# Routing moved into the attention stage: tables, routing, empty-row stores and the first expert's weights, with one block fewer

## Chip, cores and metric

One core of one Trainium2 chip. The metric is the device time in microseconds (us) of one execution of the whole kernel, given as the median of several runs.

## The reference, cut to what matters

The kernel computes one tower block for 32 sequences of 512 tokens with 256 features: an embedding lookup, a two-directional Mamba layer, then attention and a mixture of experts. The last part is what the change touches:

```
x = layer_norm(h1).reshape(-1, 256)                 # 16384 rows
top_p, top_i = top_k(softmax(x @ router_weight), 2) # 8 experts, 2 for each row
order = argsort(top_i.reshape(-1), stable=True)     # rows of an expert, in the order of tokens
within = arange(N * K) - offsets[sorted_exp]        # a row's place in its expert's list
valid = within < cap                                # cap = ceil(N * K / E * 1.25): later rows are dropped
xt = padded_tokens.reshape(E, cap, H)
fc2 = einsum('ecf,efh->ech', gelu(einsum('ech,ehf->ecf', xt, moe_w1)), moe_w2)
moe_out = zeros((N, H)).at[padded_tid].add(fc2 * padded_probs)
out = h1 + moe_out
```

## The kernel before, in words

The program is a row of blocks. In a block each engine has its own instruction stream, written out by hand, and engines meet through semaphores; at a block's end all engines meet at a barrier. The blocks are the Mamba stage, `attention_stage`, `routing_stage` and `expert_stage`.

**`attention_stage`** (from L982) goes over 32 chunks of 512 rows, unrolled in Python (attention runs along the axis of 32 sequences; a chunk is 16 of the 512 positions with their 32 rows each). GpSimd (`@block.gpsimd`) first writes masks and small tables, then computes the scales of the layer norms (`scales1`, `scales2`), normalises the attention weights, adds the residual (`base`) and sends rows (`send`): for a chunk, eight indirect DMAs that put its rows, once for each of two chosen experts, into the DRAM tensor `expert_in` (`xd_dram`), where each expert has its own region of rows. `send(c)` runs two chunks behind. SyncE (SP) loads rows of later chunks into a ring of four and stores results. TensorE's `turn2` transposes the second layer norm's rows, `router` makes the logits, and `ranks` counts how many rows before this one chose each expert. VectorE's `keep_logits`, `pick_experts`, `next_rows` and `place` work out the choice and the row in `expert_in`; `place` writes the index tile `idx`, of which there is one, so its cast (L1651) waits until the chunk before has been sent and has landed. ACT's `second_odds` makes the weight of the second choice from the logits' difference. After the last chunk a tail repeats these steps for chunks 30 and 31 with nothing left to overlap.

**`routing_stage`** (L1714) finds, from the choices of all tokens kept in `both_all`, which rows fall within an expert's capacity, and a plan: how many blocks of 512 rows each expert has, and where the rows end. GpSimd builds 128x128 tables (`same`, `later`, `below`) with 48 instructions, each waiting for the one before; TensorE multiplies them with `both_all`; VectorE scans, compares, counts (`few`), and writes `plan` and the threshold `kept`.

**`expert_stage`** fills a zero tile, stores a block of empty rows behind each expert's rows (SP, L1923, eight stores at places read from `plan`) and one behind the output (L1925), waits for all nine, and then runs the turns: for each expert so many blocks of 512 rows as the plan says, 68 in this run. A turn loads rows (L1934), transposes them, applies the layer norm's weights on ACT (`move`, L2061), splits them into a high and a low part on VectorE, multiplies with `w1` (L2022), applies gelu, multiplies with `w2` (L2034), and adds the results to the output by indirect DMA (L1983). Expert weights are loaded by GpSimd into two sets; `weights_high` rounds them on ACT, and VectorE makes the low part (L2148, L2152, L2155). Each engine keeps its own loop through `experts`, which reads the count of an expert from `plan`.

## Time and profile before

| | |
|---|---|
| median of 3 runs | 4369.67 us (4357.84 to 4372.54) |
| the profiled execution | 4369.69 us |
| its span, from the first to the last instruction | 4368.2 us |
| busy: TensorE matmul (PE), weight load (PEld) | 91%, 68% of the span |
| busy: VectorE (DVE), ScalarE (ACT), GpSimd (POOL) | 84%, 65%, 53% |
| mean granted TensorE clock | 0.906 of full speed (2.4 GHz) |

Times in the rows are microseconds from the span's start, in one profiled execution. A bracket at the end of a line tells how long the engine stood idle before the instruction, and what ended the wait. The busy shares are averages over stages that differ much; a stage has to be read by itself.

### The profile page before, as it was taken

The page shows a single profiled execution, that of the slowest core. Times are in us where ns is not written, and L with a number is a line of the kernel's source. Part 1 is how long each engine was busy: PE and PEld are TensorE (multiplying, and loading weights), DVE is VectorE, ACT ScalarE, POOL GpSimd, SP SyncE. Part 2 cuts the span into 40 slices and gives each one's busy share as a digit, 9 for nine tenths or more (in the row PEclk, how much of TensorE's full clock was granted, in tenths as well). Part 3 has the DMA queues.
Part 4 walks back from the last instruction along what each step waited for, and adds up shares of the span by engine and source line. Part 5 has one row for each costly group of instructions (what it writes and reads, how often), then busy time and mean ns, then how long its engine had stood idle before and what let it go on. Part 6 is the DMA issues. An engine that isn't in the chain of part 4 may idle for free. (4 is left out here: it accounts for less than half of the span.)

```text
span 4368.2 us, 69821 instructions
## 1 busy us (share of the span) xinstructions
PE 3962.4 (91%) x19212; PEld 2959.7 (68%) x19213; DVE 3654.4 (84%) x7005; ACT 2853.2 (65%) x4732; POOL 2325.2 (53%) x1953
## 2 busy tenths in 40 slices
PE   6999999999999999999999869999999389999998
PEld 4666566666666666666656547777877278888987
DVE  7999999999999999999999858887888356666666
ACT  5777777777777777777777746666666145554444
POOL 2454545444454545445454536666666435555555
PEclk8989989898889989898999879988899689999999
DMA  2122211221222222222222212222222155555555
GB/s 68 45 44 42 52 38 45 42 52 42 47 47 42 46 41 48 42 49 44 42 52 39 40 45 82 83 81 75 79 81 75 63 123 96 97 105 96 87 96 85
DMA packets 197949, 272.58 MB, mean 62 GB/s; under 512 B 23377, under 2 KB 142546, under 8 KB 197842
## 3 DMA queue, kind: packets, MB, share of 16 engines
q0 software_dynamic: 94720, 131.65, 17.2%
q1 hardware_dynamic: 99680, 137.43, 11.2%
q10 hardware_dynamic: 3442, 2.21, 0.2%
q8 instruction: 50, 0.82, 0.1%
q14 instruction: 57, 0.47, 0.0%
HBM read 121.07 MB, written 150.14 MB: 62 GB/s over the span
## 5 line engine op out<-in xcount | busy, mean ns | idle before, releaser
L608 PE MATMUL pj<-xt,win 128*128 128x512 f32 x3144 | 919.0, 452 | 13.6 <-DVE uc L793 10.5
L608 PEld LDWEIGHTS pj<-xt,win 128*128 128x128 f32 x3144 | 674.9, 217 | 200.2 <-issue 46.9
L1983 POOL DMA_INDIRECT out<-e_y,e_to x272 | 461.2, 1696 | 367.9 <-ACT e_y L2089 308.2
L300 POOL TENSOR_TENSOR r<-r,neg_half 128x4 f32<-128x4 f32 x64 | 90.9, 1420 | 844.5 <-ACT r L383 844.5
L793 DVE SCALAR_TENSOR_TENSOR uc<-pj,convw,uc 128x511 f32<-128x511 f32 (+2 forms) x780 | 516.8, 728 | 4.9 <-ACT uc L407 4.9
L656 PE MATMUL po<-yz,wout 128*128 128x512 f32 x1024 | 483.6, 628 | 28.3 <-ACT fb L486 28.3
L325 POOL TENSOR_TENSOR wk<-v,uc 128x512 f32<-128x512 f32 x260 | 333.0, 1281 | 246.4 <-DVE v L841 245.6
L2034 PE MATMUL e_p<-e_w,e_a 128*128 128x256 f32 x3264 | 408.7, 282 | 1.9 <-DVE e_a L2144 1.9
L656 PEld LDWEIGHTS po<-yz,wout 128*128 128x128 f32 x1024 | 198.6, 199 | 310.5 <-issue 308.6
L2022 PE MATMUL e_p<-e_xt,e_w 128*128 128x512 f32 x1632 | 390.7, 396 | 5.6 <-DVE e_w L2148 3.0
L2034 PEld LDWEIGHTS e_p<-e_w,e_a 128*128 128x128 f32 x3264 | 386.2, 188 | 12.5 <-DVE e_a L2144 6.6
L2022 PEld LDWEIGHTS e_p<-e_xt,e_w 128*128 128x128 f32 x1632 | 304.3, 190 | 71.0 <-issue 7.4
L329 POOL TENSOR_TENSOR tp<-wk,bb 128x512 f32<-128x512 f32 x260 | 332.8, 1280 | 30.5 <-POOL wk L325 19.8
L2142 DVE CAST e_a<-e_af 128x512 fp32r<-128x512 f32 x272 | 118.3, 435 | 240.2 <-ACT e_af L2082 234.4
L677 PE MATMUL po<-wfus,fo 128*128 128x256 f32 x1024 | 238.1, 386 | 75.2 <-ACT fo L477 75.2
L1218 POOL DMA_INDIRECT expert_in<-a_xs,a_idx x256 | 249.8, 976 | 94.4 <-issue 80.0
L677 PEld LDWEIGHTS po<-wfus,fo 128*128 128x128 f32 x1024 | 189.3, 190 | 151.4 <-ACT fo L477 128.2
L848 DVE TENSOR_TENSOR_SCAN tp<-y,tp 128x512 f32<-128x512 f32 x256 | 291.8, 1198 | 0.0
L2082 ACT ACTIVATE e_af<-e_p 128x512 f32<-128x512 f32 x272 | 162.3, 598 | 185.2 <-PE e_p L2022 183.9
L833 DVE SCALAR_TENSOR_TENSOR wk<-wk,lg 128x1024 f32<-128x1024 f32 x130 | 222.6, 1712 | 71.3 <-ACT lg L463 71.3
L2089 ACT ACTIVATE e_y<-e_p,e_share 128x256 f32<-128x256 f32 x272 | 114.4, 472 | 234.8 <-PE e_p L2034 234.8
L415 ACT ACTIVATE zs<-pj 128x512 f32<-128x512 f32 x260 | 155.7, 599 | 168.9 <-PE pj L608 168.9
(247 smaller groups left out, 9076.3 us busy)
## 6 DMA issues: line engine op xcount, KB each, us to landing
e_x<-expert_in SPq DMA_DIRECT2D x138, 260.0 KB, 2.6
bb<-bc SPq DMA_DIRECT2D x65, 512.0 KB, 5.3
h_rows<-fb POOLq DMA_DIRECT2D x64, 512.0 KB, 6.3
h_rows<-h0c SPq DMA_DIRECT2D x32, 512.0 KB, 2.9
a_h<-h_rows SPq DMA_DIRECT2D x128, 128.0 KB
out<-a_bs SPq DMA_DIRECT2D x128, 128.0 KB
bc<-xd SPq DMA_DIRECT2D x65, 128.0 KB, 2.2
e_w1s<-in_moe_w POOLq DMA_DIRECT2D x10, 512.0 KB, 5.8
```

The lines of the kernel that those rows point to most:

```text
L325: pool.tensor_tensor(wk[:, m, :], v[:, m, :], uc[d][:, m, :], ALU.mult).then_inc(S["dtu_ok"], 1)
L329: pool.tensor_tensor(tp[:, m, :], wk[:, m, :], bb[d][:, 0, :], ALU.mult).then_inc(S["tp_ok"], 1)
L608: i = mm(pj[m][:], win[d][wp][:, k, c:c + P], xt[xp][:, k, :], start=(k == 0 and n == 0), stop=(k == KD - 1 and n == 2))
L656: i = mm(po[k][:], wout[d][:, m, k * P:(k + 1) * P], yz[:, m, :], start=(m == 0), stop=(m == MD - 1))
L677: i = mm(po[h][:, jj * DM:(jj + 1) * DM], fo[:, k, j * P:(j + 1) * P], wfus[d][:, k, :], start=(k == 0), stop=(k == KD - 1))
L793: stt(uc[d][:, m, to], pj[m][:, of], convw[d][:, m, tap:tap + 1], uc[d][:, m, to], ALU.mult, ALU.add).then_inc(S["cv"], 1)
L833: stt(wk[:, mm, :], wk[:, mm, :], 1.0, lg[:, mm, :], ALU.subtract, ALU.subtract).then_inc(S["g_ok"], 1)
L848: nc.vector.tensor_tensor_scan(tp[:, m, step], y[:, m, step], tp[:, m, step], 0.0, ALU.mult, ALU.add).then_inc(S["h_ok"], 1)
L1218: pool.indirect_dma_start(out=xd_dram, out_offset=bass.IndirectOffsetOnAxis(ap=idx[:, k, j:j + 1].bitcast(U32), axis=0), in_=xs[c % SENDS] ...
L1983: pool.indirect_dma_start(out=out, out_offset=bass.IndirectOffsetOnAxis(ap=to[n][:, j:j + 1].bitcast(U32), axis=0), in_=y[n][:, j, :], in_ ...
L2022: o = mm(p1[m][:], w1[i][wp][:, k, m * P:(m + 1) * P], xt[xp][:, k, :], start=(k == 0 and s == 0), stop=(k == KD - 1 and s == 2))
L2034: o = mm(p2[n][:, j, :], a[ap][:, m, (n * HT + j) * P:(n * HT + j + 1) * P], w2[i][wp][:, m, :], start=(m == 0 and s == 0), stop=(m == MF ...
```

## The change

The routing block is gone. Its parts go into the attention block, and some of what the expert block did first goes there too. The tiles that both blocks use (`plan`, `expert`, `kept`, the identity, the zero tile, both sets of weights) and a semaphore `emptied` are now made once outside and passed in as `moe`.

- GpSimd builds the routing tables and fills the zero tile after the first two calls of `scales1`. The constant rows that VectorE wrote one column at a time become two iotas. The identity is shared: the copies that the routing and the expert block built are gone.
- SP loads expert 0's weights after slot 2, and stores the empty block behind the output after slot 3 and waits for it. After its last slot it stores the eight empty blocks, as soon as the plan is there, and waits for the first of them; the other seven are waited for in the expert block, before expert 1's rows are read.
- ACT rounds expert 0's weights at the end of its stream.
- TensorE and VectorE: `ranks(30)` comes ahead of the last `turn2`, and `next_rows(30)`, `place(30)` ahead of `keep_logits(31)`. The routing products follow `ranks(31)`, and VectorE's routing follows `place(31)`, with the plan made before the scans. The first expert's low half is made there.
- The expert block starts without those steps. GpSimd loads only expert 1's weights there.

```diff
         @block.sync
+            def expert_weights():
+                for dst, name, of in ((moe.w1s, "moe_w1", "(k p) f -> p k f"), (moe.w2s, "moe_w2", "(m p) c -> p m c")):
+                    rows = DM if name == "moe_w1" else FF
+                    sp.dma_start(dst[0][:], w[name][0:rows, :].rearrange(of, p=P)).then_inc(S["ld_e"], 16)
+
+            def empty_rows():
+
+                sp.wait_ge(S["plan_ok"], 1)
+                for e in range(NE):
+                    row = sp.value_load(moe.plan[0:1, 1, e:e + 1], min_val=0, max_val=NE * X_ROWS - PAIR)
+                    sp.dma_start(xd_dram[bass.ds(row, PAIR), :].rearrange("(p j) c -> p j c", p=P), moe.zero[:]
+                                 ).then_inc(S["zst"] if e == 0 else moe.emptied, 16)
             for c in range(NCH + 1):
                 slot(c)
+                if c == 2:
+                    expert_weights()
+                if c == 3:
+                    sp.wait_ge(S["tab"], TABLES_R)
+                    sp.dma_start(out[NSEQ * SEQ:NSEQ * SEQ + PAIR, :].rearrange("(p j) c -> p j c", p=P),
+                                 moe.zero[:, :, 0:DM]).then_inc(S["zst"], 16)
+                    sp.wait_ge(S["zst"], 16)
+            empty_rows()
+            sp.wait_ge(S["zst"], 32)
+            sp.wait_ge(S["ld_e"], 32)
...
         @block.gpsimd
             scales1(0)
             scales1(1)
+            routing_tables()
...
         @block.scalar
             second_odds(NCH - 1)
+            act.wait_ge(S["ld_e"], 32)
+            act.activation(moe.w1[0][0][:], moe.w1s[0][:], ACT.Copy).then_inc(S["hi_ok"], 1)
+            act.activation(moe.w2[0][0][:], moe.w2s[0][:], ACT.Copy).then_inc(S["hi_ok"], 1)
...
         @block.tensor
+            ranks(NCH - 2)
             turn2(NCH - 1, True)
-            ranks(NCH - 2)
+            pe.wait_ge(S["rt"], ROUTES * (NCH - 2) + PICKS + 2)
             router(NCH - 1)
             pe.wait_ge(S["lg_ok"], NCH)
-            pe.wait_ge(S["rt"], ROUTES * (NCH - 2) + PICKS + 2)
             ranks(NCH - 1)
+            def routing():
+                pe.wait_ge(S["tab"], TABLES_R)
+                pe.wait_ge(S["rt"], ROUTES * (NCH - 1) + PICKS)
+                pe.wait_ge(S["hh_ok"], 2 * NCH)
+                pe.wait_ge(S["x2t_ok"], KD * NCH)
+                flat = both_all[:].rearrange("p t e -> p (t e)")
+                for i in range(2):
+                    cols = slice(SEQ * i, SEQ * (i + 1))
+                    mm(A[i][:], same[:], flat[:, cols], start=True, stop=True)
+                    mm(A[2 + i][:], later[:], flat[:, cols], start=True, stop=True)
+                pe.wait_ge(S["tot_ok"], 1)
+                mm(B[0][:, 0:NE], below[:], total[:], start=True, stop=True)
+                mm(B[0][:, NE:2 * NE], onef[:], total[:], start=True, stop=True).then_inc(S["counted"], 1)
+                pe.wait_ge(S["few_ok"], 1)
+                mm(B[1][:, 0:NE], onef[:], few[:], start=True, stop=True).then_inc(S["kept_ps"], 1)
...
         @block.vector
             normalise2(NCH - 1)
-            keep_logits(NCH - 1)
             next_rows(NCH - 2)
             place(NCH - 2)
+            keep_logits(NCH - 1)
             pick_experts(NCH - 1)
             next_rows(NCH - 1)
             place(NCH - 1)
+            def routing():
+                nc.vector.tensor_reduce(total[:], both_all[:].rearrange("p t e -> p e t"), AX_X, ALU.add
+                                        ).then_inc(S["tot_ok"], 1)
...
+                nc.vector.tensor_copy(moe.plan[:], planf[:]).then_inc(S["plan_ok"], 1)
...
 def expert_stage
         @block.sync
-            sp.wait_ge(S["zeroed"], 2)
-
-            for e in range(NE):
-                row = sp.value_load(plan[0:1, 1, e:e + 1], min_val=0, max_val=NE * X_ROWS - PAIR)
...
-            sp.wait_ge(S["zst"], 16 * (NE + 1))
+            def all_emptied(pair, i, q):
+
+                if i == 1:
+                    sp.wait_ge(emptied, 16 * (NE - 1))
...
         @block.gpsimd
-            load_weights(0, 0)
             load_weights(1, 1)
...
         @block.scalar
-            weights_high(0, 1)
             for n in range(2):
                 move(0, n)
...
         @block.vector
-            dve.wait_ge(S["hi_ok"], 1)
-            tt(w1[0][1][:], w1s[0][:], w1[0][0][:].bitcast(F32), ALU.subtract).then_inc(S["w1_ok"], 1)
+            dve.nop().then_inc(S["w1_ok"], 1)
```

The new function on GpSimd; the part left out is the 42 copies, multiplications and selects of before, each of which waits for the one ahead:

```
            def routing_tables():
                n = 0
                for tile, value in ((same, 0.0), (later, 0.0), (below, 0.0), (onef, 1.0)):
                    pool.memset(tile[:], value).then_inc(S["tab"], 1)
...
                pool.iota(row0[:], [[X_ROWS, NE]], base=0, channel_multiplier=0,
                          allow_small_or_imprecise_dtypes=True).then_inc(S["tab"], 1)
                pool.iota(steps[:], [[PAIR, MAX_PAIRS - 1]], base=PAIR, channel_multiplier=0,
                          allow_small_or_imprecise_dtypes=True).then_inc(S["tab"], 1)
                pool.memset(zero[:], 0.0).then_inc(S["tab"], 1)
                n += 3
                pool.wait_ge(S["tab"], n)
                pool.iota(zero[:, :, TOKEN], [[1, PAIR // P]], base=NSEQ * SEQ, channel_multiplier=PAIR // P,
                          allow_small_or_imprecise_dtypes=True).then_inc(S["tab"], 1)
```

The end of VectorE's routing, after the scans and additions that make `rank`:

```
                nc.vector.tensor_reduce(few[:], inside[:].rearrange("p t e -> p e t"), AX_X, ALU.add
                                        ).then_inc(S["few_ok"], 1)
                dve.wait_ge(S["hi_ok"], 1)
                tt(moe.w1[0][1][:], moe.w1s[0][:], moe.w1[0][0][:].bitcast(F32), ALU.subtract).then_inc(S["low_ok"], 1)
                dve.wait_ge(S["kept_ps"], 1)
                ts(moe.kept[:], inside_of, -0.5, None, ALU.add).then_inc(S["seq"], 1)
```

## Rows read from the trace of the kernel before

**Rows 1.** Stretches: length; busy PE, PEld, DVE, ACT, POOL (instructions); PE clock, DMA share, GB/s.

```profile
2524.00:3410.00 886.00, 815.47 (x5375) 676.89 (x5376) 711.49 (x2471) 550.78 (x957) 549.01 (x591) 0.90 0.22 75
3410.00:3516.41 106.41, 17.49 (x88) 13.11 (x88) 26.31 (x139) 8.79 (x14) 38.38 (x80) 0.56 0.29 103
3516.41:3531.40 14.99, 14.99 (x80) 13.01 (x81) 9.21 (x23) 5.50 (x11) 2.05 (x3) 0.79 0.31 102
3531.40:4340.00 808.60, 803.68 (x5271) 722.08 (x5270) 543.24 (x1465) 404.32 (x806) 458.30 (x278) 1.00 0.57 95
```

**Rows 2.** Timeline, tail of the attention block: start, length, engine, line, operation.

```profile
3421.15 0.19 ACT L1308 ACTIVATE a_odds<-a_gap 128x4 f32<-128x4 f32 x1
...
3425.54 0.16 DVE L1642 TENSOR_SCALAR a_whole<-a_odds 128x4 f32<-128x4 f32 x1
...
3427.17 1.06 POOL L1218 DMA_INDIRECT expert_in<-a_xs,a_idx  x1 [6.27 <-DVE a_flag L1613]
...
3438.66 0.17 DVE L1651 CAST a_idx<-a_dest 128x8 int32<-128x8 f32 x1 [7.53 <-DMA expert_in<-a_xs,a_idx]
...
3438.96 0.16 DVE L1658 TENSOR_TENSOR a_xs<-a_first,a_xs 128x4 f32<-128x4 f32 x1
3439.90 0.96 POOL L1218 DMA_INDIRECT expert_in<-a_xs,a_idx  x1 [2.81 <-DVE a_xs L1658]
...
3448.75 0.96 POOL L1218 DMA_INDIRECT expert_in<-a_xs,a_idx  x1 [0.30 <-issue]
```

**Rows 3.** One line's instructions: GpSimd's queue at the attention block's end (ns, start).

```profile
L995 POOLq DRAIN  x1: 2506/2506/2506, 3451.4 to 3451.4; - x1
```

**Rows 4.** Timeline of the routing block.

```profile
3454.20 1.98 DVE L1792 TENSOR_REDUCE r_total<-both_all 128x8 f32<-128x1024 f32 x1 [15.08 <-PEq L995]
...
3468.37 2.08 PE L1781 MATMUL r_ps<-both_all,r_same 128*128 128x512 f32 x2 [38.26 <-POOL r_below L1769]
...
3473.39 0.28 PE L1784 MATMUL r_pb<-r_total,r_below 128*128 128x8 f32 x2
...
3474.01 1.53 DVE L1810 TENSOR_TENSOR_SCAN r_rank<-r_ones,r_ps 128x64 f32<-128x64 f32 x8 [16.77 <-PE r_pb L1785]
...
3482.82 0.41 DVE L1832 TENSOR_TENSOR r_over<-r_pb,r_steps 128x248 f32<-128x248 f32 x1
...
3483.97 0.16 DVE L1843 CAST plan<-r_planf 1x16 int32<-1x16 f32 x1
3484.05 0.15 DVE L1846 TENSOR_SCALAR kept<-r_pk 128x8 f32<-128x8 f32 x1
```

**Rows 5.** Timeline of the expert block up to its first product.

```profile
3484.70 0.96 POOL L1948 MEMSET e_zero<- 128x1040 f32 x1 [16.38 <-POOLq L1719]
...
3486.70 1.23 POOL L1957 DMA_DIRECT2D e_ln<-in_ln  x2 [0.24 <-issue]
3486.86 10.91 SPq L1923 DMA_DIRECT2D expert_in<-e_zero  x8
...
3491.41 1.28 ACT L2054 ACT_TABLE_LOAD   x1 [61.93 <-DMA e_ln<-in_ln]
...
3498.01 1.23 DVE L2155 TENSOR_TENSOR e_w<-e_w1s,e_w 128x1024 fp32r<-128x1024 f32 x1 [13.81 <-ACT e_w L2067]
3508.96 6.83 SPq L1934 DMA_DIRECT2D e_x<-expert_in  x4
...
3512.93 1.93 ACT L2061 ACTIVATE e_xf<-e_pt,e_ln 128x256 f32<-128x256 f32 x4 [14.00 <-PE e_pt L2003]
...
3516.41 8.64 PE L2022 MATMUL e_p<-e_xt,e_w 128*128 128x512 f32 x24 [2.67 <-DVE e_xt L2136]
```

**Rows 6.** Timeline of GpSimd at the start of the attention block.

```profile
2570.35 4.10 POOL L1204 TENSOR_TENSOR a_ss<-a_ss,a_rs 128x512 f32<-128x512 f32 x4 [24.43 <-DVE a_rs L1551]
```

**Rows 7.** DMA issues from 3480 to 3520: count, size, median us to landing.

```profile
expert_in<-e_zero SPq DMA_DIRECT2D x8, 520.0 KB, 9.1
...
e_w2s<-in_moe_w POOLq DMA_DIRECT2D x3, 512.0 KB, 8.3
```

More of the change, by code:

```diff
@@ L11 @@
 import numpy as np
+from collections import namedtuple
 from contextlib import ExitStack
@@ L981, with attention_stage @@
 TABLES = 11 + NQ + 2 + 2 * NE + NQ
-NT = NSEQ * SEQ // P
+NTILE = NSEQ * SEQ // P
+FF = 512
+MF = FF // P
+CAP = -(-NSEQ * SEQ * TOP * 5 // (NE * 4))
+HALF = 256
+HT = HALF // P
+MAX_PAIRS = NSEQ * SEQ // PAIR
+TABLES_R = 4 + 16 + 10 + 16 + 4
+ExpertTiles = namedtuple("ExpertTiles", "plan expert kept ident zero emptied w1s w2s w1 w2")
 MASKED = -2.0 ** 127
-def attention_stage(nc, w, h1_dram, out, xd_dram, both_all):
+def attention_stage(nc, w, h1_dram, out, xd_dram, moe):
     ctx = ExitStack()
@@ L1038, in attention_stage @@
         lgc = sb("a_lgc", [P, TT, NE])
-        expert = sb("a_expert", [P, NE])
+        expert = moe.expert
         seen = sb("a_seen", [P, NE])
@@ L1058, in attention_stage @@
         xs = [sb(f"a_xs{i}", [P, TT, XW]) for i in range(SENDS)]
+        block_shape = [P, NTILE, NE]
+        both_all = sb("r_both", block_shape)
+        same = sb("r_same", [P, P])
+        later = sb("r_later", [P, P])
+        below = sb("r_below", [P, P])
+        onef = sb("r_ones", [P, P])
+        row0 = sb("r_row0", [P, NE])
+        steps = sb("r_steps", [P, MAX_PAIRS - 1])
+        rank = sb("r_rank", block_shape)
+        inside = sb("r_inside", block_shape)
+        total = sb("r_total", [P, NE])
+        few = sb("r_few", [P, NE])
+        over = sb("r_over", [P, NE, MAX_PAIRS - 1])
+        turns = sb("r_turns", [P, NE])
+        planf = sb("r_planf", [1, 2, NE])
+        zero = moe.zero
         A = [ctx.enter_context(nc.psum_tensor(f"a_pa{i}", [P, SEQ], F32)) for i in range(4)]
@@ L1718, in routing_stage, with expert_stage @@
+            routing()
+def expert_stage(nc, w1_dram, w2_dram, lnw_dram, xd_dram, out, moe):
     ctx = ExitStack()
@@ L1721, in sb @@
             return ctx.enter_context(nc.sbuf_tensor(name, shape, dt))
-        block_shape = [P, NTILE, NE]
-        ident = sb("r_ident", [P, P])
-        same = sb("r_same", [P, P])
-        later = sb("r_later", [P, P])
-        below = sb("r_below", [P, P])
-        ones = sb("r_ones", [P, P])
-        row0 = sb("r_row0", [P, NE])
-        steps = sb("r_steps", [P, MAX_PAIRS - 1])
-        rank = sb("r_rank", block_shape)
-        inside = sb("r_inside", block_shape)
-        total = sb("r_total", [P, NE])
@@ L1734, in routing_stage @@
-        few = sb("r_few", [P, NE])
-        over = sb("r_over", [P, NE, MAX_PAIRS - 1])
-        turns = sb("r_turns", [P, NE])
-        planf = sb("r_planf", [1, 2, NE])
-        ps_same = [ctx.enter_context(nc.psum_tensor(f"r_ps{i}", [P, SEQ], F32)) for i in range(2)]
-        ps_part = [ctx.enter_context(nc.psum_tensor(f"r_pp{i}", [P, SEQ], F32)) for i in range(2)]
-        ps_base = ctx.enter_context(nc.psum_tensor("r_pb", [P, 2, NE], F32))
-        ps_kept = ctx.enter_context(nc.psum_tensor("r_pk", [P, NE], F32))
@@ L1775, in _ @@
-        @block.tensor
-        def _(pe):
-            pe.wait_ge(S["tab"], TABLES_R)
-            flat = both_all[:].rearrange("p t e -> p (t e)")
-            for i in range(2):
-                cols = slice(SEQ * i, SEQ * (i + 1))
-                nc.tensor.matmul(ps_same[i][:], same[:], flat[:, cols], start=True, stop=True)
-                nc.tensor.matmul(ps_part[i][:], later[:], flat[:, cols], start=True, stop=True)
-            pe.wait_ge(S["tot_ok"], 1)
-            nc.tensor.matmul(ps_base[:, 0, :], below[:], total[:], start=True, stop=True)
-            nc.tensor.matmul(ps_base[:, 1, :], ones[:], total[:], start=True, stop=True).then_inc(S["counted"], 1)
-            pe.wait_ge(S["few_ok"], 1)
-            nc.tensor.matmul(ps_kept[:], ones[:], few[:], start=True, stop=True).then_inc(S["kept_ps"], 1)
@@ L1851 @@
-TABLES_R = 6 + 16 + 10 + 16
-def expert_stage(nc, w1_dram, w2_dram, lnw_dram, xd_dram, out, plan, expert, kept):
-    ctx = ExitStack()
-    with ctx:
-        def sb(name, shape, dt=F32):
-            return ctx.enter_context(nc.sbuf_tensor(name, shape, dt))
-        ident = sb("e_ident", [P, P])
+        plan, expert, kept, ident, zero, emptied, w1s, w2s, w1, w2 = moe
         ln = sb("e_ln", [P, 2, KD])
-        w1s = [sb(f"e_w1s{i}", [P, KD, FF]) for i in range(2)]
-        w2s = [sb(f"e_w2s{i}", [P, MF, DM]) for i in range(2)]
-        w1 = [[sb(f"e_w1{i}{h}", [P, KD, FF], F32R) for h in range(2)] for i in range(2)]
-        w2 = [[sb(f"e_w2{i}{h}", [P, MF, DM], F32R) for h in range(2)] for i in range(2)]
@@ L2076, in weights @@
                 act.wait_ge(S["f2_ps"], 2 * q + 2)
-                weights_high(1 - i, pair + i + 1)
+                weights_high(1 - i, pair + 1)
             def gelu(q, m):
```

210 lines of the change are left out of this document (92 added, 118 removed).

## The prediction

> **What bounds the kernel now.** I read the busy time by stretches first [rows 1]. TensorE is busy 815 of 886 us in the attention stage's chunks and 804 of 809 us in the expert turns, so neither has slack that a moved table could give back. Between them lies a hole: from 3410.00 to 3516.41 TensorE works 17.5 of 106.4 us, and no other engine is near full either (GpSimd, the busiest, has 38.4). A hole in which nothing is full is a chain of waits, so it has to be read instruction by instruction, and the sum below follows that chain. Its end is the first expert product at 3516.41; after it the same 68 turns follow, so whatever moves that product moves the end.
>
> The chain of before has five links. (1) VectorE places chunk 30's rows only after chunk 31's logits, so the eight indirect stores of chunk 30 start at 3427.17, and since chunk 31's index tile is the same tile, its cast waits until they have landed, 3438.66; eight more stores then run to 3449.71 [rows 2]. (2) GpSimd needs 2.5 us to drain at the block's end [rows 3], and the routing block starts at 3454.20. (3) GpSimd builds the tables while TensorE waits 38.3 us for them, to 3468.37 [rows 4]. (4) Products, scans, counts and the plan take until 3484.20 [rows 4]. (5) In the expert block the zero tile is filled, eight empty blocks are stored and all must land before the first rows are read at 3508.96 [rows 5].
>
> **The change part by part.** All times below are microseconds in the profiled execution.
>
> *Tables.* 14.2 us of GpSimd work (3454.20 to 3468.37, [rows 4]) go, with small additions (two iotas, the zero tile's 0.96 [rows 5], one more iota; the second and third identity tiles and 47 VectorE memsets fall away), to the place after the first two scales of the attention stage. There GpSimd idles 24.43 us before 2570.35 [rows 6]. About 15 + 1 us fit, with some 8 to spare, so I cost them at nothing. Uncovered, as much of the 16 as sticks out would delay the first chunk's normalising once.
>
> *SP's early transfers.* Two weight loads after chunk slot 2 and one zero store plus its wait after slot 3. Behind them on SP stand only the next chunk's row loads and results. A chunk takes 886/32 = 27.7 us, the DMA engines are 22% busy there [rows 1], and half-megabyte transfers landed in 8.3 to 9.1 us even in the crowded stretch [rows 7]; the ring of input rows is loaded three chunks ahead. Nothing; if the cover failed, one slot late by under 10 us. ACT's two rounding copies come after its last chunk 31 exponential, where it has nothing else.
>
> *Reordered ranking.* The ranks of chunk 30 now run on TensorE before the last transposes, and its rows are placed before chunk 31's logits. What is late next is the weight pair from the exponential, which ACT does after its two copies: it ends at 3421.34 [rows 2]. From that step to the first store is 3427.17 - 3425.54 = 1.63 [rows 2], so chunk 30's stores start at 3423.0, 4.2 earlier. The new TensorE wait before the last router product holds that product and the last ranks, and waits for two short additions that VectorE does right after its normalised rows; the router product waits for ACT's two copies anyway, which end just before the exponential. The logits' path is not delayed, since placing then ends before the router does. The chain of stores keeps its lengths: 3423.0 + 11.5 (first store to the cast) = 3434.5; VectorE is through placing 0.5 later, 3435.0; chunk 31's stores start at 3435.7 and end 9.8 later, 3445.5 [rows 2].
>
> *Routing inside the block.* VectorE is in order, so the sum over tokens starts only at 3435.0, behind that cast; but the four large products depend on the counts alone and have run meanwhile. Sum 1.98, to 3437.0. The four small products took 0.62 from their first start to the scan [rows 4]; TensorE will have idled, so I take twice that: 3438.2. The plan now comes first: 1.31 (3482.82 to 3484.13 [rows 4]), to 3439.5. From here three engines run side by side:
> SP reads a plan entry (I take 1.2, near one eighth of the 10.91 that eight rounds took [rows 5]) and issues eight stores in 10.91: 3451.6. It waits for the first of them alone.
> VectorE does the scans and counts, 8.81 (3474.01 to 3482.82), the first expert's low half 1.23 and the last threshold 0.15 [rows 4, 5]: 3449.7.
> GpSimd sees its last store land 1.7 after its end (3449.71 to the drain at 3451.4), 3447.2, and drains 2.5 [rows 2, 3]: 3449.7.
> SP is last. The stores' issue costs between what the next engine allows (3449.7) and 3451.6; I keep the latter, since these are the same eight rounds. What they collide with is the landing of chunk 31's last stores; the DMA engines are 29% busy over the hole [rows 1], and GpSimd has 2 us to give before it would be last.
>
> *The expert block.* The barrier took 0.5 (3484.20 to 3484.70 [rows 4, 5]): start at 3452.1. GpSimd has no fills left and issues the layer-norm rows at 3452.3. ACT's table load started 4.71 after that issue (3486.70 to 3491.41) and lasts 1.28 [rows 5]: 3458.3. The row path: 1.4 for one plan read and issue (10.91/8), then 3.97 from issue to ACT's first copy (3508.96 to 3512.93 [rows 5]): 3457.5, just ahead. So ACT's table decides, where the zero stores decided before. From the copy to the first product 3.48 (3512.93 to 3516.41): 3461.8. Expert 1's weights are issued only now, about 3454, and land 8.3 later [rows 7], 3462.4. Queued behind ACT's wait for them are the first turn's activations, due about 3 us into the product, so the two 1-us copies just fit; a few us more would be made up, because the product lasts 8.64 at a clock not yet full [rows 1, 5] and only its last activation is needed before the second product.
>
> **Sum:** 3516.4 - 3461.8 = 54.6 saved. The profiled execution took 4369.69 (span 4368.2), practically the median of the runs shown, 4369.67: 4369.7 - 54.6 = 4315.1.
>
> Where a page speaks against this: GpSimd's stores were evenly 0.96 long with VectorE idle (3439.90 to 3449.71) and beside its small picks [rows 2], but the long scans never ran beside them in this trace. The Trainium skill, "SBUF — State Buffer", section "SBUF: two separate sides", says that VectorE and GpSimd share a port pair that certain VectorE operations lock for their whole length, so that GpSimd can't write DMA descriptors meanwhile. By the row the sum stays 4315; by the rule it is the third rival below. No stretch of before shows the two together.
>
> **The rivals.**
> *Forecast*, about 4315; its own range 4309 to 4321.
> *The rows queue behind the empties.* The empty stores are still landing when the expert block starts: before, a store took 9.1 from issue to landing [rows 7]. The last is issued at about 3451.3 and lands by 3460.4; rows that land no earlier than as if issued then give 3460.4 + 3.97 + 3.48 = 3467.9, 6.1 late, at most 4321. For it: the same SP queue. Against: the 9.1 was taken beside four weight loads, which are mostly gone. The Trainium skill, "DMA: Bandwidth & Descriptors", section "Queues, rings and completion order", says that a ring's descriptors are consumed in order; by that rule this case is the one to expect if stores pile up.
> *VectorE holds up GpSimd's last stores.* At 3439.5 five of eight are left; if each waits for a scan or an add of 1.2 to 2 us, the last ends 8 later, GpSimd drains at 3457.7 and the block ends 6 later: 4321.
> *Reordering gives nothing* (the exponential or the ranks come later than I read): 4.2 lost, 4319.
> *Slower: the clock.* The turns have a granted clock of 1.00, the chunks 0.90 [rows 1]. Were the hole what earns the turns full clock, then at 0.90 they would take 808.6/0.90 = 898, 90 longer: 4405. It decides where the turns' clock is under 808.6/(808.6 + 54.6) = 0.937. Against: the clock stood at 0.56 in the hole and 0.79 in the first turn [rows 1]: it comes back with work, not with rest.
>
> **How the numbers follow.** Chances: forecast 0.72, queue 0.10, held-up stores 0.06, no gain from reordering 0.05, clock 0.02; 0.05 remains for a cover that fails in the chunks, half of it small, half big enough to lose the gain. Two runs' executions shown differ by up to 14.7 (4357.84 to 4372.54), so the same kernel can come out some 12 lower; 0.3% (13 us) is about what a measurement of this kernel can tell from no change. Low end: 4315 less 11; high end: the 4321 cases with a few us of spread, 4324. Faster by over 0.3% (below 4356.6): all but the clock and half of the remainder, 0.95; same 0.02; slower 0.03.
>
> **What would show it.** Right: GpSimd's tables before the first chunk's normalising at unchanged time; chunk 30's first indirect store near 3423; eight empty stores issued while chunk 31's stores run; one barrier in the hole; the first product near 3462; turns of unchanged length. Wrong: ACT's first copy waiting for rows rather than for its table load (queue); chunk 31's stores further apart than 1.27 (port); a turn clock under 1.00; first chunk later than 2570; or chunks longer than 27.7.

## The result, and the profile after

The changed kernel took 4337.13 us (median of 5 runs, 4330.87 to 4339.85); the kernel before took 4369.67 beside it (4357.84 to 4373.39). The ratio is 0.9922, its 95% interval 0.9912 to 0.9933. It is faster, by 32.5 us and not by the 54.6 forecast, and 4337 lies above the range. The profiled execution took 4339.85, its span is 4338.3.

Windows by stretch of the kernel after, cut at the same points of the program as [rows 1], with the same columns:

```profile
2524.00:3424.24 900.24, 840.08 (x5375) 703.13 (x5376) 709.97 (x2471) 550.07 (x957) 559.99 (x640) 0.87 0.22 75
3424.24:3477.08 52.84, 19.26 (x89) 13.46 (x88) 27.51 (x92) 8.54 (x14) 24.59 (x26) 0.59 0.50 180
3477.08:3491.79 14.71, 14.71 (x81) 12.87 (x82) 9.21 (x23) 5.79 (x11) 2.27 (x3) 0.83 0.31 97
3491.79:4310.00 818.21, 815.57 (x5271) 728.81 (x5270) 543.55 (x1465) 403.37 (x806) 468.40 (x278) 1.00 0.57 94
```

The second line is the hole: 106.41 has become 52.84, as forecast. But the two long stretches beside it, which the sum left alone, have grown. The chunks take 900.24 instead of 886.00 for the same 5375 TensorE instructions, at a granted clock of 0.87 instead of 0.90. The turns take 818.21 instead of 808.60 for the same 5271 instructions, at 1.00 both times.

The timeline of the hole after (start, length, engine, line, operation), to be held against [rows 2, 4, 5]:

```profile
3435.39 0.19 ACT L1393 ACTIVATE a_odds<-a_gap 128x4 f32<-128x4 f32 x1
...
3437.27 1.06 POOL L1267 DMA_INDIRECT expert_in<-a_xs,a_idx  x1 [2.14 <-DVE a_xs L1766]
...
3448.75 0.17 DVE L1759 CAST a_idx<-a_dest 128x8 int32<-128x8 f32 x1 [4.79 <-DMA expert_in<-a_xs,a_idx]
...
3449.24 1.98 DVE L1813 TENSOR_REDUCE r_total<-r_both 128x8 f32<-128x1024 f32 x1
...
3453.54 0.16 DVE L1831 CAST plan<-r_planf 1x16 int32<-1x16 f32 x1
3453.62 1.51 DVE L1839 TENSOR_TENSOR_SCAN r_rank<-r_ones,a_pa 128x64 f32<-128x64 f32 x8
3453.77 0.96 POOL L1267 DMA_INDIRECT expert_in<-a_xs,a_idx  x1 [0.30 <-issue]
3454.91 11.16 SPq L1153 DMA_DIRECT2D expert_in<-r_zero  x8
3455.04 0.96 POOL L1267 DMA_INDIRECT expert_in<-a_xs,a_idx  x1 [0.30 <-issue]
3455.17 2.02 DVE L1839 TENSOR_TENSOR_SCAN r_rank<-r_ones,r_rank,a_pa 128x64 f32<-128x64 f32 x8
3456.30 0.96 POOL L1267 DMA_INDIRECT expert_in<-a_xs,a_idx  x1 [0.30 <-issue]
...
3458.83 0.96 POOL L1267 DMA_INDIRECT expert_in<-a_xs,a_idx  x1 [0.30 <-issue]
...
3467.33 1.18 POOL L1958 DMA_DIRECT2D e_ln<-in_ln  x2 [7.54 <-POOLq L1004]
3468.49 0.73 POOL L1961 DMA_DIRECT2D e_w1s<-in_moe_w  x1
3468.65 6.82 SPq L1942 DMA_DIRECT2D e_x<-expert_in  x4
...
3469.97 1.28 ACT L2055 ACT_TABLE_LOAD   x1 [25.52 <-DMA e_ln<-in_ln]
...
3472.61 1.02 ACT L2062 ACTIVATE e_xf<-e_pt,e_ln 128x256 f32<-128x256 f32 x2 [1.36 <-PE e_pt L2003]
...
3473.59 1.11 PE L2003 MATMUL e_pt<-ident,e_x 128*128 128x128 f32 x4 [1.01 <-DMA e_x<-expert_in]
...
3477.08 1.22 PE L2022 MATMUL e_p<-e_xt,e_w 128*128 128x512 f32 x2 [2.38 <-DVE e_xt L2136]
```

The tail starts 14.24 us later than before, because the chunks ended later: the last chunk's first output projection starts at 3423.52, before at 3409.28. With 14.24 added, the forecast's points are 3437.24 for the first store of chunk 30 (measured 3437.27), 3449.24 for the sum over tokens (3449.24), 3453.74 for the end of the plan (3453.54 + 0.16), 3465.84 for the end of SP's stores (3454.91 + 11.16 = 3466.07) and 3476.04 for the first expert product (3477.08). The chain in the hole was read rightly to about a microsecond.

One line's instructions, GpSimd's queue at the block's end, is as in [rows 3]:

```profile
L1004 POOLq DRAIN  x1: 2508/2508/2508, 3463.7 to 3463.7; - x1
```

GpSimd at the start of the attention block, timeline, against [rows 6]:

```profile
2545.33 0.19 POOL L1275 MEMSET r_same<- 128x128 f32 x1
...
2560.18 0.14 POOL L1302 IOTA r_zero<- 128x4 f32 x1
...
2568.90 4.10 POOL L1253 TENSOR_TENSOR a_ss<-a_ss,a_rs 128x512 f32<-128x512 f32 x4 [8.58 <-DVE a_rs L1659]
```

The tables take 15.0 us in the gap and leave 8.58 of idle time, where 8 were forecast; the first normalising is no later (2568.90, before 2570.35).

**Four stages.** For what follows the span is cut at three marks that every trace has: *chunks* run from the first residual sum (`a_bs`) on GpSimd to the last chunk's first output projection, the *hole* from there to the first expert product, the *turns* from there to the end. What comes between the attention block's first table (`a_nh`) and the first mark is *chunk 0*.

| kernel | chunk 0 | chunks | hole | turns | span |
|---|---|---|---|---|---|
| before | 66.75 | 818.57 | 107.13 | 851.81 | 4368.22 |
| after | 65.42 | 834.26 | 53.56 | 861.23 | 4338.31 |
| difference | -1.33 | +15.69 | -53.57 | +9.42 | -29.91 |

(Ahead of chunk 0 the two differ by 0.13.) So 53.6 us were gained in the hole, and 25.1 were given back in stages where the forecast had set nothing. The experiments ask why.

**The chunks have two lengths.** From one `a_bs` to the next, a chunk of either kernel takes about 25.9 or 27.33 us. Windows of the kernel before: all chunks from the first mark to the last `a_bs`, a short chunk, a stretch inside the short one, a long chunk, and a stretch inside the long one.

```profile
2590.72:3418.55 827.83, 776.60 (x5177) 648.97 (x5176) 686.44 (x2401) 523.00 (x914) 533.34 (x545) 0.91 0.22 77
2747.39:2773.24 25.85, 23.77 (x169) 20.21 (x168) 22.81 (x80) 16.93 (x30) 17.58 (x18) 0.93 0.24 83
2754.58:2758.00 3.42, 3.42 (x18) 3.09 (x17) 3.28 (x22) 2.80 (x5) 0.44 (x2) 0.50 0.26 86
2905.21:2932.55 27.34, 26.44 (x172) 22.27 (x171) 22.53 (x80) 17.23 (x31) 17.57 (x18) 0.88 0.22 78
2911.60:2918.42 6.82, 6.82 (x33) 6.49 (x33) 5.15 (x32) 4.76 (x7) 2.92 (x5) 0.50 0.26 88
```

Windows of the kernel after: all chunks in the same way, one of them, a stretch inside it.

```profile
2589.26:3432.78 843.52, 802.44 (x5191) 676.93 (x5190) 685.08 (x2402) 522.32 (x914) 532.78 (x544) 0.88 0.23 78
2830.55:2857.89 27.34, 26.45 (x172) 22.28 (x171) 22.63 (x80) 17.22 (x31) 17.57 (x19) 0.88 0.23 78
2836.92:2843.75 6.83, 6.83 (x33) 6.50 (x34) 5.13 (x31) 4.75 (x7) 2.79 (x5) 0.50 0.28 96
```

In a long chunk the granted clock stands at 0.50, the lower of its two levels (1.2 GHz), for 6.8 us, a stretch that begins within the router products, just after TensorE has waited for ACT's transposed rows (in the kernel after at 2836.92; the products start at 2835.74 after 0.89 of waiting, as a line further down shows). The short chunk shown has that wait too, and a longer one, and its clock falls for 3.4 us only, at 2754.58:

```profile
2752.09 1.95 PE L1453 MATMUL a_pb<-a_wr,a_x2t 128*128 128x8 f32 x16 [2.08 <-ACT a_x2t L1302]
```

So the wait alone does not make a chunk long. Of before, the intervals 12 to 23 and 30 are long and 5, 11 and 29 in between (26.85); after, all from the fourth to the thirtieth are long. (The sixteenth takes about 30 in every kernel.)

### The profile page after: what moved, and what is told of

It is laid out like the page before. It is cut to its first block and busy times, and to the rows that moved or that the text cites. A ratio compares the mean times of both kernels' runs of the same rounds, so it can differ in the third digit from the quotient of the medians.

```text
span 4338.3 us, 69764 instructions
## 1 busy us (share of the span) xinstructions
PE 4001.3 (92%) x19212; PEld 2993.2 (69%) x19213; DVE 3654.2 (84%) x6958; ACT 2850.2 (66%) x4732; POOL 2333.2 (54%) x1949
## 5 line engine op out<-in xcount | busy, mean ns | idle before, releaser
L1983 POOL DMA_INDIRECT out<-e_y,e_to x272 | 471.8, 1734 | 366.8 <-ACT e_y L2089 306.1
L657 PE MATMUL po<-yz,wout 128*128 128x512 f32 x1024 | 483.6, 628 | 28.1 <-ACT fb L487 28.1
```

The source lines that it names most:

```text
L657: i = mm(po[k][:], wout[d][:, m, k * P:(k + 1) * P], yz[:, m, :], start=(m == 0), stop=(m == MD - 1))
L1983: pool.indirect_dma_start(out=out, out_offset=bass.IndirectOffsetOnAxis(ap=to[n][:, j:j + 1].bitcast(U32), axis=0), in_=y[n][:, j, :], in_ ...
```

## The experiments

Two questions: is it the moved work that lengthens the chunks, or only the clock; and what lengthens the turns at full clock.

**First for the chunks: spare products while TensorE waits.** Before the router's wait, six products go into columns of the logits' bank that nobody reads then, in both kernels.

```diff
             def router(c):
+                for _ in range(6):
+                    mm(B[3][:, P:SEQ], ident[:], wq[:, 0, :, :].rearrange("p t e -> p (t e)"), start=True, stop=True)
                 pe.wait_ge(S["x2t_ok"], KD * (c + 1))
```

> The changed kernel, with six more products of 128x384 in each chunk, into columns of a PSUM bank that nobody reads, placed ahead of the router products where TensorE waits for ACT's copies. Theory 1 (the chunks of the changed kernel are longer because TensorE's granted clock falls to half in every chunk there, and which chunks do so is a matter of phase): the clock stays up, the chunks go from 27.33 to about 25.9 us, 28 x 1.4 = 40 us off, about 4297. Theory 2 (the moved work itself slows the chunks, through SP's early transfers or tables): the products fill idle time only, chunks stay at 27.3, 4337 or slower.

> The kernel before, with the same six products in each chunk. Theory 1: its chunks are at 27.33 us in about half of the cases (chunks 11 to 23, 29, 30), so some 17 x 1.4 = 24 us go, about 4346, and all chunks stand at about 25.9; the distance to the changed kernel with the same products then shows the change without the clock's dips, 44 (53.6 at the hole, less 9.4 in the turns). Theory 2: no change or slower, 4370 or above, and the distance stays 32.

Measured: 4340.6 (4339.81 to 4341.43; ratio to the kernel before 0.9925, 0.9909 to 0.9942) and 4384.48 (4382.32 to 4385.41; 1.0032, 1.0021 to 1.0043).

| kernel | chunk 0 | chunks | hole | turns | span |
|---|---|---|---|---|---|
| after_fill | 66.39 | 832.83 | 54.17 | 860.65 | 4338.34 |
| before_fill | 64.97 | 833.63 | 110.77 | 846.25 | 4380.85 |

Windows of after_fill, all chunks as above:

```profile
2590.69:3433.31 842.62, 830.85 (x5563) 652.96 (x5562) 679.26 (x2402) 519.16 (x914) 534.67 (x544) 0.99 0.23 78
```

Neither time is the one that theory 1 gave (4297 and 4346), but the distance of the two medians, 43.9, is (44, against 32 by theory 2). The clock no longer falls in steady chunks, but six products cost as much as the clock did: every steady chunk takes about 27.2. That makes the two kernels equal there, 832.8 against 833.6. The work that the change moved into the chunks costs them nothing. The turns still differ, by 14.

**The address of the tiles.** The change makes the expert weights outside the blocks, so the layer-norm tile `e_ln` now lies between them and the tiles of the expert block, and everything sits elsewhere in SBUF, the on-chip memory that holds the tiles. Spacers move tiles and change no instruction.

The first, after_pad, is the kernel after with 32 bytes more ahead of the row tiles:

```diff
         ln = sb("e_ln", [P, 2, KD])
+        pad = sb("e_pad", [P, 8])
         x = [sb(f"e_x{i}", [P, HT, XW]) for i in range(2)]
```

The second, before_skew, is the kernel before with as much (a tile takes multiples of 32 bytes) at the same place:

```diff
         w2 = [[sb(f"e_w2{i}{h}", [P, MF, DM], F32R) for h in range(2)] for i in range(2)]
+        pad = sb("e_pad", [P, 4])
         x = [sb(f"e_x{i}", [P, HT, XW]) for i in range(2)]
```

> The changed kernel, with one tile of 32 bytes a partition more between the expert weights and the rows' tiles, so that weights and activations have the same start modulo 64 bytes, as in the kernel before. Theory A (the turns are longer because the expert tiles lie at other addresses): turns go back from 12.33 to 12.16 us, 68 x 0.17 = 11 off, about 4326. Theory B (the turns' pace is a matter of how TensorE's stream fell into step, or of something else): turns stay at 12.33, 4337.

> The kernel before, with one tile of 32 bytes a partition more at the same place, so that weights and activations differ by 32 modulo 64 bytes, as in the changed kernel. Theory A: turns go from 12.16 to 12.33 us, about 4380. Theory B: turns stay at 12.16, 4370.

Measured: 4326.28 (4313.35 to 4335.59; 0.9896, 0.9866 to 0.9926) and 4382.51 (4365.74 to 4390.21; 1.0028, 1.001 to 1.0047).

| kernel | chunk 0 | chunks | hole | turns | span |
|---|---|---|---|---|---|
| after_pad | 65.68 | 810.36 | 53.64 | 861.31 | 4316.09 |
| before_skew | 65.24 | 804.67 | 109.18 | 860.17 | 4364.27 |

Half hit, half miss. Moving the row tiles by 32 bytes slows the turns of the kernel before to those of the kernel after; but the spacer in the kernel after, with which weights and rows all start on multiples of 64, does not bring its turns back. The median of after_pad, 4326.28, is the number that theory A gave (4326), but by luck: the gain is in its chunks, not in its turns. That weights and rows must both start 32 bytes past a multiple of 64, as in the kernel before, was still open. The chunks say more than was asked of them: 810.4 and 804.7 with not one instruction of the attention stage changed. Without spare products their length differs from kernel to kernel by up to 30 us, and it goes with the granted clock: 0.88 in the kernel after, 0.91 in the kernel before, 0.93 in before_skew, whose window over all chunks is

```profile
2590.24:3404.18 813.94, 757.48 (x5177) 629.64 (x5176) 687.41 (x2401) 521.51 (x914) 532.94 (x544) 0.93 0.23 79
```

**Addresses again, the reordering, and fewer spare products.** after_match puts 32 bytes ahead of the weights and 32 behind them; before_addr gives the kernel before the very addresses of the kernel after; after_order undoes the reordered ranking of chunks 30 and 31 alone; after_fill2 is after_match with two spare products instead of six.

The spacers of after_match, in `build` (the call that makes the tiles is split for them; those lines are left out):

```diff
             emptied=ctx.enter_context(nc.semaphore("r_emptied")),
...
+        pad1 = sb("e_pad1", [P, 8])
             w1s=[sb(f"e_w1s{i}", [P, KD, FF]) for i in range(2)],
...
             w2=[[sb(f"e_w2{i}{h}", [P, MF, DM], F32R) for h in range(2)] for i in range(2)])
+        pad2 = sb("e_pad2", [P, 8])
         attention_stage(nc, h, h1_dram, out, xd_dram, moe)
```

Those of before_addr, in `expert_stage`:

```diff
+        pad1 = sb("e_pad1", [P, 8])
         w1s = [sb(f"e_w1s{i}", [P, KD, FF]) for i in range(2)]
...
+        pad2 = sb("e_pad2", [P, 8])
         x = [sb(f"e_x{i}", [P, HT, XW]) for i in range(2)]
```

after_order, on TensorE and on VectorE:

```diff
-            ranks(NCH - 2)
             turn2(NCH - 1, True)
-            pe.wait_ge(S["rt"], ROUTES * (NCH - 2) + PICKS + 2)
+            ranks(NCH - 2)
             router(NCH - 1)
             pe.wait_ge(S["lg_ok"], NCH)
+            pe.wait_ge(S["rt"], ROUTES * (NCH - 2) + PICKS + 2)
             ranks(NCH - 1)
...
+            keep_logits(NCH - 1)
             next_rows(NCH - 2)
             place(NCH - 2)
-            keep_logits(NCH - 1)
```

after_fill2, beside the spacers of after_match:

```diff
             def router(c):
+                for _ in range(2):
+                    mm(B[3][:, P:SEQ], ident[:], wq[:, 0, :, :].rearrange("p t e -> p (t e)"), start=True, stop=True)
```

> The changed kernel with two 32-byte spacer tiles, one ahead of the expert weights and one behind them, so that weights start 32 bytes past a multiple of 64 (as in the kernel before) while every other tile keeps its place modulo 64. By the theory that the turns' pace hangs on where weights and rows start, the 68 turns go back from 861.2 to 847 to 853 us (a steady turn from 12.33 to about 12.1, the second products 114 ns apart instead of 117 to 118). By the rival (the turns are slow because of what runs ahead of them, or of the moved first weights) they stay at 859 to 862. Hole 53 to 55 by both. Chunks anywhere from 804 to 834 by both, since nothing in them is changed; so the time 4302 to 4333 by the first, 4312 to 4342 by the rival.

> The kernel before with two 32-byte spacer tiles in the expert block alone, ahead of the weights and ahead of the row tiles, which puts weights, rows and activations at the very addresses of the changed kernel (weights on a multiple of 64, the others 32 past one). By the theory of the addresses the turns take 859 to 862 instead of 851.8; by the rival 846 to 852. Hole 106 to 111 by both. Time 4375 to 4395 by the first, 4357 to 4380 by the rival (chunks 804 to 834).

> The changed kernel with only the reordered ranking of the last two chunks undone, on TensorE and on VectorE. By the prediction's step the first store of chunk 30 comes 4.2 us later after the last chunk's projection than in the changed kernel, and the hole grows from 53.6 to 57.8. By the rival (the reordering gives nothing, the exponential and the ranks come as late anyway) the hole stays at 53 to 54.5; turns 861 by both, chunks 804 to 834 by both.

> As after_match, and in each chunk TensorE does two instead of six spare products of 384 columns while it waits for ACT ahead of the router products. If the chunks' pace is set by whether the granted clock falls inside them, and two products keep it up, chunks come out at 25.9 to 26.4 us each: 795 to 815 in all, with no granted clock near a half in steady chunks. If two are too few, the pace has the same two values as without them, 804 to 834 in all. If the pace is set by the work that the change moved in, the clock's pieces may go and the chunks stay near 834. Turns as in after_match.

| kernel | time | ratio to before | chunks | hole | turns |
|---|---|---|---|---|---|
| after_match | 4340.48 | 0.9915 (0.9898 to 0.9931) | 834.12 | 53.36 | 861.60 |
| before_addr | 4388.98 | 1.0020 (1.0010 to 1.0031) | 827.25 | 109.86 | 860.91 |
| after_order | 4334.15 | 0.9897 (0.9880 to 0.9913) | 823.95 | 57.63 | 860.51 |
| after_fill2 | 4301.33 | 0.9823 (0.9807 to 0.9839) | 796.41 | 53.77 | 861.19 |

after_order: the hole grows by 4.07; the step was forecast at 4.2. Its median is none the worse for it, because its chunks happened to be 10 us shorter: a step of 4 us can't be seen in these medians, only in the stage. Its timeline of GpSimd has the first store of chunk 30 behind chunk 31's flags again, as in [rows 2]:

```profile
3431.10 1.06 POOL L1267 DMA_INDIRECT expert_in<-a_xs,a_idx  x1 [6.28 <-DVE a_flag L1721]
```

after_fill2: two products are enough. The timeline of TensorE in one chunk of the kernel after, and then in one of after_fill2:

```profile
2835.74 2.54 PE L1542 MATMUL a_pb<-a_wr,a_x2t 128*128 128x8 f32 x16 [0.89 <-ACT a_x2t L1387]
```

```profile
2905.62 0.49 PE L1539 MATMUL a_pb<-a_wq,ident 128*128 128x384 f32 x1
2906.84 1.95 PE L1544 MATMUL a_pb<-a_wr,a_x2t 128*128 128x8 f32 x16 [0.74 <-ACT a_x2t L1387]
```

Windows of after_fill2, one chunk, and all chunks as above:

```profile
2954.25:2980.13 25.88, 25.64 (x177) 19.91 (x176) 22.66 (x80) 17.31 (x31) 17.59 (x18) 1.00 0.24 84
2592.11:3397.78 805.67, 777.42 (x5315) 625.80 (x5314) 688.13 (x2402) 522.60 (x914) 534.49 (x544) 0.96 0.24 81
```

TensorE does 124 instructions more in the same chunks and is through 37.9 us sooner (805.67 against 843.52), at 0.96 instead of 0.88: the clock still falls now and then, but no longer in every chunk. The pace is the clock's.

after_match and before_addr: the theory of a start 32 bytes past a multiple of 64 falls, since after_match has it for all tiles and keeps the long turns. But before_addr shows that the addresses of the kernel after, in the kernel before, are enough to bring them. What the kernels with short turns share is then not where the tiles start modulo 64, but how far the rows of the first product (`e_xt`) lie above its first weights (`e_w1`), worked out from the sizes of the tiles between: 41,024 bytes of each partition in before and before_fill (eight weight tiles of 4,096 bytes, two row tiles of 2,080 and two of 2,048); 41,056 in after, after_order, after_fill, before_skew and before_addr; 41,088 in after_pad, after_match and after_fill2. The 32 bytes of `e_ln` are the first difference. The activations of the second product (`e_a`) lie behind `e_xt`, so they moved away from their weights by as much.

**The distance.** after_same puts all expert tiles exactly 4,096 bytes above their places in the kernel before; after_same_fill2 adds the two spare products; before_fill2 has these in the kernel before. after_ln_fill2 has no spacer and moves only `e_ln` behind the other tiles, which restores the distance but not where the tiles start.

In `build` (after_same and after_same_fill2; again without the lines that split the call):

```diff
+        pad = sb("e_pad", [P, 1016])
             w1s=[sb(f"e_w1s{i}", [P, KD, FF]) for i in range(2)],
```

In `expert_stage` (these two and after_ln_fill2):

```diff
-        ln = sb("e_ln", [P, 2, KD])
         x = [sb(f"e_x{i}", [P, HT, XW]) for i in range(2)]
...
         to = [sb(f"e_to{i}", [P, HT], I32) for i in range(2)]
+        ln = sb("e_ln", [P, 2, KD])
```

> The changed kernel with one spacer tile of 4,064 bytes ahead of the expert weights and the layer-norm tile moved behind the other expert tiles, so that every expert tile from the first staged weights to the last stands exactly 4,096 bytes above its place in the kernel before, whose distances to each other it has again (rows of the products 41,024 bytes above the weights; the changed kernel has 41,056, the kernel with two small spacers 41,088). If the turns' pace hangs on where these tiles stand to each other, the 68 turns come back to 845 to 853 us (a steady turn about 12.1). If it hangs on something else that the change brought (the order of the work ahead, the longer program), they stay at 859 to 862. Hole 53 to 54.5 and chunks 804 to 834 by both: 4300 to 4333, against 4312 to 4342.

> The same with the two spare products per chunk that held the granted clock up. Chunks 794 to 800, hole 53 to 54.5 by every theory. With turns of 845 to 853 the time is 4287 to 4297 and the lowest of all; with turns at 859 to 862 it is that of the earlier kernel with two spare products, 4300 to 4305.

> The kernel before with the same two spare products per chunk. If the chunks' pace is the clock's alone, the chunks take 794 to 800 us here too, though nothing of the change is in them; if the moved work had cost them anything, the two kernels with spare products would differ by it. Turns 845 to 853, hole 106 to 111: a time of 4342 to 4352. The kernel after_same_fill2 less this one is then the change by itself: 53 to 56 us by the prediction's sum if the turns come back there, 40 to 47 if not.

> The changed kernel with the two spare products per chunk, no spacer, and the layer-norm tile moved behind the other expert tiles: rows of the products again 41,024 bytes above the weights, as in the kernel before, but weights and rows each 32 bytes past their place in it, both on a multiple of 64. If the distance between the tiles alone sets the turns' pace, they take 846 to 853 us and the time is 4285 to 4296. If where each tile starts matters too, they take 859 to 862, and the time is 4300 to 4305.

| kernel | time | ratio to before | chunks | hole | turns | span |
|---|---|---|---|---|---|---|
| after_same | 4325.35 | 0.9882 (0.9866 to 0.9899) | 831.62 | 53.48 | 848.71 | 4323.53 |
| after_same_fill2 | 4288.18 | 0.9795 (0.9778 to 0.9811) | 798.24 | 53.58 | 849.78 | 4292.88 |
| before_fill2 | 4346.52 | 0.9930 (0.9913 to 0.9946) | 793.67 | 110.00 | 851.90 | 4344.72 |
| after_ln_fill2 | 4287.32 | 0.9822 (0.9798 to 0.9845) | 796.54 | 53.61 | 848.21 | 4287.52 |

The turns come back with the distance, wherever the tiles start. The medians of after_same_fill2 and before_fill2 lie 58.3 apart, a little more than the 53 to 56 expected. Windows of before_fill2, all chunks as above:

```profile
2589.15:3392.60 803.45, 776.93 (x5301) 624.43 (x5300) 688.80 (x2401) 521.70 (x914) 533.50 (x544) 0.96 0.23 80
```

Now the turns. Windows from the second turn's first product to the last turn's, 66 turns each, in this order: before, after, before_addr, after_match, after_same, after_ln_fill2.

```profile
3531.47:4341.46 809.99, 805.07 (x5282) 723.47 (x5281) 543.92 (x1466) 404.32 (x806) 458.98 (x279) 1.00 0.57 95
```

```profile
3491.79:4311.38 819.59, 816.95 (x5283) 730.19 (x5281) 544.00 (x1466) 403.37 (x806) 469.26 (x279) 1.00 0.57 94
```

```profile
3539.98:4360.02 820.04, 816.92 (x5282) 730.53 (x5281) 544.71 (x1466) 403.93 (x806) 459.49 (x279) 1.00 0.56 94
```

```profile
3491.40:4311.34 819.94, 817.46 (x5282) 734.53 (x5281) 543.19 (x1466) 403.49 (x806) 470.81 (x279) 1.00 0.56 94
```

```profile
3488.96:4296.80 807.84, 804.19 (x5282) 723.37 (x5281) 543.14 (x1466) 403.57 (x806) 460.63 (x279) 1.00 0.57 95
```

```profile
3453.77:4260.77 807.00, 803.78 (x5283) 722.48 (x5281) 542.58 (x1466) 403.41 (x806) 461.11 (x279) 1.00 0.57 96
```

The reader is to see three things: the clock is 1.00 in all; the instructions are the same, but for a record or two; and TensorE is busy throughout, so the 10 to 13 us lie in the products themselves and not in waits between them. Two lengths come out, 807 to 810 and 820, and they follow the distance. The eight kernels not shown fit: 806 to 810 for the three with 41,024 bytes, 819 to 820 for the five with more.

The same windows for the products with `w1` alone (tile `e_xt`), in the kernels before, after and after_match, and then for those with `w2` alone (tile `e_a`):

```profile
3531.47:4341.46 809.99, 376.36 (x1584) 1.00 0.57 95
3491.79:4311.38 819.59, 381.38 (x1585) 1.00 0.57 94
3491.40:4311.34 819.94, 379.55 (x1584) 1.00 0.56 94
```

```profile
3531.47:4341.46 809.99, 396.83 (x3170) 1.00 0.57 95
3491.79:4311.38 819.59, 403.65 (x3170) 1.00 0.57 94
3491.40:4311.34 819.94, 405.95 (x3170) 1.00 0.56 94
```

Both products take longer, the second more than the first, and with 41,056 bytes (after) the 12 us are split between them otherwise than with 41,088 (after_match).

after_ln_fill2 beats both kernels: its median lies 78 us below that of the kernel before beside it (4365.71) and 50 below the kernel after, which was measured on another occasion.

## Why the prediction was right and wrong

**Right: the hole.** Forecast 54.6, measured 53.6. The tables hide in GpSimd's gap; the reordering gives 4.1 (after_order) for 4.2; SP's eight stores took 11.16 for 10.91 and were through at 3466.07, and GpSimd's drain was through at 3466.2 (3463.7 + 2.51), so the two that the prediction had to choose between came out even; two drains and a barrier became one. The agreement to 1.0 us is in part luck: in its four variants here the kernel before has holes of 109.2 to 110.8, not 107.1. In the expert block two errors of opposite sign remain. ACT's table load, taken as the bound with 4.71 from GpSimd's issue, began 2.64 after it (3467.33 to 3469.97); so the rows decided, from issue to ACT's copy in 3.96 for 3.97. (A first copy that waits for rows was the prediction's sign of the queue; here it came of the early table load.) But between barrier and issue SP took 1.95 (3466.7 to 3468.65) instead of 1.4, and the second half of the rows came late enough that TensorE waited 1.01 for it at 3473.59: copy to product took 4.47 for 3.48.

**Rivals that did not come.** The rows did not queue behind the empties: the empty stores landed 3.6 us after issue (median of DMA issues in the hole), where 9.1 had been feared:

```profile
expert_in<-r_zero SPq DMA_DIRECT2D x8, 520.0 KB, 3.6
```

Only the 1.01 at the second half may be of that kind, or of the weights of expert 1, which GpSimd sent off at 3468.49, just ahead of the rows; no run tells the two apart. GpSimd's stores stayed 1.27 apart (3453.77, 3455.04, 3456.30) beside VectorE's scans. The shared port pair that the Trainium skill tells of ("SBUF — State Buffer", section "SBUF: two separate sides") left no mark there; whether these scans are among the operations that it means, no run shows. The turns' clock is 1.00, so the slower rival is out as well.

**Wrong: "neither has slack", taken to mean that neither can change.** The failed step is the one at the head of the prediction: "after it the same 68 turns follow, so whatever moves that product moves the end", with "a chunk takes 886/32 = 27.7 us" as a fixed size. Stages that are full of TensorE work have no slack to give, but their length still hangs on what one TensorE instruction takes, and both were different in the changed kernel. The prediction's own sign, chunks longer than 27.7, came: 900.24/32 = 28.1.

*The chunks, +15.7.* The 27.7 is no chunk's length but a mean over chunks of 25.9 and 27.33 us and the first stretch, and the clock of 0.90 in [rows 1] was its sign: a clock between two levels means that some of the time is spent at the lower one. Taken chunk by chunk, that row would have shown that the kernel before stood half in a state that could be lost or won. Interval by interval, eleven went from short to long (15.2 us), three from between to long (1.5) and the third from short to between (0.9); the first is 1.5 shorter (24.25 for 25.75), and the rest give back 0.4: 15.7. That it is the clock, not the moved work, is shown by the kernels with spare products, where the two kernels' chunks come out equal (832.8 and 833.6 with six; 796.5 and 793.7 with two, where before_fill2's hole is 2.9 longer than that of before instead). The Trainium skill ("TensorE: Matmul & The Clock Gate", section "HAM oscillation — how this bites in real kernels") describes a loop in which a wait lets the clock fall anew in every round. The long chunks here agree in kind; the wait there is for a DMA, here for ACT. The short ones do not: they have the wait (2.08 at 2752.09), and the one shown of before spends 3.4 us at the lower clock, the next none (1.00 from 2758.00 to 2805.78).

*The turns, +9.4.* The new layout of tiles was not priced at all; the diff was read for instructions alone. `e_ln`, 32 bytes, went between the weights and the rows, and 66 turns took 819.59 instead of 809.99 at full clock; with the distance put back they took 807.00 to 808.4.

*The range* reached 11 us down for differences from run to run and only a few up. The same spread, 4357.84 to 4372.54, speaks for both sides.

With both effects held equal, the change is worth about what was forecast, 54.6: after_ln_fill2 less before_fill2 is 57.2 us in the spans (53.5 in chunks and hole together, 3.7 in the turns), and after_same_fill2 less before_fill2 is 58.3 in the medians, 51.8 in the spans.

**Open.** Why 32 bytes between two operands lengthen a product, and which of the moved tiles it is (rows, activations and all behind them moved together). What decides, without spare products, which chunks of a run are long: the kernels without spare products had 804.7 to 834.3. So whether the change itself brings the long chunks, or only the way in which its runs fell, is not shown. That the runs of one kernel spread by up to 22 us fits other shares of long chunks, and the mean granted clock of each run goes with it (after_pad: 4313.35 at 0.915, 4317.62 at 0.914, 4334.94 at 0.907, 4335.59 at 0.906), but only the profiled execution shows its chunks.

## What to carry to other kernels

Before setting a stage to "unchanged", look at it in slices: a mean clock between the two levels may mean, as it did here, that its length can change without a change in its work. Here two spare products per chunk, while TensorE waited for ACT, were worth some 38 us, more than half as much as the whole change to the hole. When a diff moves tiles, compare the distances between the operands of the busiest instruction, and measure stages, not only ends: a gain of 4 us is plain in its stage and invisible in the median.

## What the runs showed of the hardware

- A loop with the same instructions ran at two paces, 25.9 and 27.33 us a round, and kept each for ten rounds and more; in the slower one the granted clock stood at 0.50 for 6.8 us of a round (1.2 GHz) and at 1.00 else, in the faster one for 3.4 us (at 2754.58 of the kernel before) or not at all (the round after it, 1.00 from 2758.00 to 2805.78).
- More work made it faster: 124 more instructions on TensorE, 37.9 us less.
- Products of the same shapes at a granted clock of 1.00 took 806 to 810 us for 66 turns in the six kernels with 41,024 bytes from weights to rows, and 819 to 820 in the eight with 41,056 or 41,088.
- Eight stores of 520 KB landed in 3.6 us each, two and a half times as fast as when four weight loads ran beside them (9.1, [rows 7]).
